# Softmax attention scores from float32r parts in two row tiles, in place of bfloat16 parts over the whole array

## The reference, cut to what matters

```python
q, k, v = split(x @ qkv_w.T + qkv_b)            # 16 heads, HD = 8
scores  = einsum('bhqe,bhke->bhqk', q, k) / sqrt(8)
attn    = softmax(scores, axis=-1)              # over 2048 keys
out     = einsum('bhqk,bhke->bhqe', attn, v)
out     = out.reshape(b, s, d) @ proj_w.T + proj_b
```

## Time and profile before

| | us |
|---|---|
| runs shown, median of 3 | 1872.74 (1870.85 to 1875.92) |
| the profiled execution | 1868.55 |
| its span in the trace | 1866.7 |
| mean granted TensorE clock | 0.928 of full |
| PE busy in the span | 1628.6 (87%) |
| DVE busy | 1353.9 (73%) |
| ACT busy | 837.3 (45%) |

### The profile page before, as it was taken

One profiled execution on the slowest core, in us unless ns is written; L12 is line 12 of the kernel. 1 busy time (PEld: TensorE's weight loads), 2 busy tenths in 40 slices (PEclk: granted clock), 3 DMA queues, 4 the chain that ended last, 5 costly groups with the idle time before them and its releaser, 6 DMA issues. The chain is left out here.

```text
span 1866.7 us, 21571 instructions
## 1 busy us (share of the span) xinstructions
PE 1628.6 (87%) x7272; PEld 684.2 (37%) x7285; DVE 1353.9 (73%) x1951; ACT 837.3 (45%) x1493; POOL 222.5 (12%) x145
## 2 busy tenths in 40 slices
PE   6987589999999999999998888899994446589999
PEld 3433212222222222222221533366661112256665
DVE  5776788888888888888870686656657999745654
ACT  2433427767767667677677343322223000042222
POOL 2222300000000000000000022211101324301110
PEclk8998659999999999999999899899996777799999
DMA  6000410012001110011000000000000000000000
GB/s 169 3 0 1 123 29 8 15 27 40 8 10 31 27 21 6 27 27 23 2 1 2 1 0 0 0 1 1 0 1 0 0 1 0 1 1 6 6 6 6
DMA packets 32016, 29.42 MB, mean 16 GB/s; under 512 B 7788, under 2 KB 27032, under 8 KB 31928
## 3 DMA queue, kind: packets, MB, share of 16 engines
q1 hardware_dynamic: 31928, 28.31, 6.1%
HBM read 22.13 MB, written 4.19 MB: 14 GB/s over the span
## 5 line engine op out<-in xcount | busy, mean ns | idle before, releaser
L1382 DVE TENSOR_REDUCE mx<-ps 128x1 f32<-128x1024 f32 x512 | 604.5, 1220 | 134.2 <-PE ps L1269 130.8
L1269 PE MATMUL ps<-k,q 72*128 72x512 bf16 x1024 | 401.9, 407 | 26.7 <-PEq L967 14.9
L1304 PE MATMUL ps<-q,k 84*128 84x512 bf16 x1024 | 344.4, 382 | 14.6 <-ACT xn L1359 11.7
L1359 ACT ACTIVATE xT<-ps 128x512 f32<-128x512 f32 x512 | 265.2, 601 | 149.6 <-PE ps L1304 149.6
L1359 ACT ACTIVATE xn<-ps 128x512 f32<-128x512 f32 x512 | 266.2, 601 | 102.5 <-PE ps L1304 102.5
L1269 PEld LDWEIGHTS ps<-k,q 72*128 72x128 bf16 x1024 | 109.6, 115 | 333.0 <-DVE mx L1382 184.4
L854 ACT ACTIVATE silu<-ps 128x512 f32<-128x512 f32 x144 | 85.3, 596 | 265.2 <-PE ps L827 261.9
L1304 PEld LDWEIGHTS ps<-q,k 84*128 84x128 bf16 x1024 | 102.5, 102 | 171.1 <-ACT xn L1359 63.4
L889 DVE TENSOR_TENSOR hid<-ps,silu 128x512 f32<-128x512 f32 x144 | 97.8, 689 | 91.1 <-PE ps L831 89.4
L827 PE MATMUL ps<-xT,ew 128*128 (+1 forms) x288 | 151.0, 606 | 6.5 <-PEq L1750 4.8
L817 PEld LDWEIGHTS ps<-ew,hid 128*128 128x128 f32 x1152 | 138.7, 192 | 30.6 <-issue 29.9
(11 more groups left out here) (238 smaller groups left out, 1686.4 us busy)
## 6 DMA issues: line engine op xcount, KB each, us to landing
k<-k_parts SPq DMA_DIRECT2D x90, 64.0 KB
q<-q_parts SPq DMA_DIRECT2D x144, 32.0 KB
k<-k_parts SPq DMA_DIRECT2D x108, 32.0 KB
ew<-in_L_ffn_w_dram SPq DMA_DIRECT2D x2, 1024.0 KB
wraw<-in_L_ffn_w_dram SPq DMA_DIRECT2D x3, 512.0 KB, 6.8
q_parts<-part SPq DMA_DIRECT2D x4, 384.0 KB, 4.3
k_parts<-part SPq DMA_DIRECT2D x4, 384.0 KB, 2.6
v<-values SPq DMA_DIRECT2D x8, 144.0 KB, 5.0
```

Source lines behind the costliest of these rows:

```text
L1269: mm = nc.tensor.matmul(m.ps[:, S1B[i % 4], :], queries, k1[:, h, kc * CHUNK:(kc + 1) * CHUNK], start=True, stop=True)
L1304: nc.tensor.matmul(m.ps[:, S2_BANK[s], :], k2[:, h, kt * P:(kt + 1) * P], q[:, qc, h, :], start=True, stop=True).then_inc(s2_ready, 1)
L1359: nc.scalar.activation(ex[kt % P_RING][:, h, :], m.ps[:, S2_BANK[s], :], ACT.Exp).then_inc(exped, 1)
L1382: nc.vector.reduce_max(mx[:, h, qt, kc:kc + 1], m.ps[:, 2 * (i % 2):2 * (i % 2) + 2, :], AX.XY)\
```

## The change

Queries and keys are split into two float32 parts: the value with its low 12 bits cleared (`bitwise_and` with -4096), and the rest. A head then needs 4 products of parts, 32 rows, and 8 further rows carry the maxima (two parts of four heads). They are kept as float32r. Two heads lie in one tile: one at partitions 0 to 39, the other at 64 to 103 (ROW_TILE = 64), so a first pass is a pair of matmuls into two banks, one in either half of the array's rows, and one `reduce_max` with two outputs takes both. Scores of even heads use the lower rows, those of odd heads the upper ones. The maxima are split in two parts on DVE; 8 DMAs take them instead of 4.

The order on PE is new: scores stand three steps ahead of the tile's `weigh`, which now takes the tile's own exponentials, and first passes come as pairs in 32 places a unit (LEAD = 8 places, HOLE = 1). During the start 14 further matmuls on zeros (`warm`) stand between first passes. In the parts stage DVE clears the bits, POOL subtracts, and ACT no longer copies; eight one-column `affine_select`s make `own_row` at its start.

```diff
-LEAD = 12
-HOLE = 3
+LEAD = 8
+HOLE = 1
-    q = m.sb("q", [ROWS_M, CHUNKS, GH, CHUNK], BF16, stack=kv_stack)
-    k1 = m.sb("k1", [ROWS, GH, T], BF16, stack=kv_stack)
+    q = m.sb("q", [P, CHUNKS, PAIRED, CHUNK], F32R, stack=kv_stack)
+    k1 = m.sb("k1", [P, PAIRED, T], F32R, stack=kv_stack)
...
+            for h in range(GH):
+                for i in range(PARTS2):
+                    row = h % 2 * ROW_TILE + ROWS + i * GH + h
+                    own(nc.gpsimd.affine_select(out=own_row[:, h // 2:h // 2 + 1], ...
+            for n in range(len(jobs)):
+                low_part(n)      # POOL: full - high part, float32, 512 columns
...
-        S2_BANK = [S2B[s % 3] for s in range(STEPS - 1)] + [S2B[1]]
+        SLOTS = 2 * TILES
+        done = [max(0, (k + 1 - HOLE) * PAIRS // (SLOTS - HOLE)) for k in range(-1, SLOTS)]
+        S1_IN = [range(done[k], done[k + 1]) for k in range(SLOTS)]
...
+            def load_maxima(u):
+                sp.wait_ge(max_turned, u + 1)
+                for b in range(P // 32):
+                    rows = neg_turned[b * 32:b * 32 + PARTS2 * GH, :, :].rearrange("r j t -> r (j t)").unsqueeze(1)\
+                        .to_broadcast([PARTS2 * GH, PAIRED, P])
+                    for p in range(2):
+                        at = p * ROW_TILE + ROWS
+                        sp.dma_start(q[at:at + PARTS2 * GH, u % CHUNKS, :, b * P:(b + 1) * P].bitcast(F32), rows)\
+                            .then_inc(max_loaded, 16)
...
+            def first_pass(u, i):
+                g, qc = u // CHUNKS, u % CHUNKS
+                kc, qt, pair = i // (PAIRS // CHUNKS), i // 2 % TPC, i % 2
...
+                if u > 0 or i >= 2:
+                    pe.wait_ge(s1_used, u * PAIRS + i - 1)
+                for p in range(2):
+                    rows = slice(p * ROW_TILE, p * ROW_TILE + ROWS)
+                    queries = q[rows, qc, pair, :].rearrange("r (p t) -> r t p", t=TPC)[:, qt, :]
+                    mm = nc.tensor.matmul(m.ps[:, S1B[2 * pair + p], :], queries, k1[rows, pair, kc * CHUNK:(kc + 1) * CHUNK],
+                                          start=True, stop=True)
+                mm.then_inc(s1_ready, 1)
...
+            def score(n):
+                u, s = n // STEPS, n % STEPS
+                g, qc, kt, h = u // CHUNKS, u % CHUNKS, s // GH, s % GH
+                if s == 0:
+                    pe.wait_ge(max_loaded, DMAS_M * (u + 1))
...
+                if n >= len(S2B):
+                    pe.wait_ge(exped, n - len(S2B) + 1)
+                rows = slice(h % 2 * ROW_TILE, h % 2 * ROW_TILE + ROWS_M)
+                nc.tensor.matmul(m.ps[:, S2B[n % len(S2B)], :], k2[rows, h // 2, kt * P:(kt + 1) * P], q[rows, qc, h // 2, :],
+                                 start=True, stop=True).then_inc(s2_ready, 1)
...
+            for i in range(PAIRS):
+                first_pass(0, i)
+            for i in range(S1_IN[LEAD].start):
+                warm()
+                warm()
+                first_pass(1, i)
+            pe.wait_ge(own_stored, 4)
+            for n in range(len(S2B)):
+                score(n)
+            for u in range(UNITS):
                 for kt in range(TILES):
+                    n = u * STEPS + kt * GH
+                    score(n + 3)
+                    ahead(u, 2 * kt)
+                    score(n + 4)
+                    score(n + 5)
+                    score(n + 6)
+                    ahead(u, 2 * kt + 1)
+                    weigh(u, kt)
...
-                    nc.vector.reduce_max(mx[:, h, qt, kc:kc + 1], m.ps[:, 2 * (i % 2):2 * (i % 2) + 2, :], AX.XY)\
+                    nc.vector.reduce_max(mx[:, 2 * pair:2 * pair + 2, qt, kc], m.ps[:, 2 * pair:2 * pair + 2, :], AX.X)\
                         .then_inc(s1_used, 1)
```

More of the change, by code:

```diff
@@ L6 @@
 BF16 = mybir.dt.bfloat16
+F32R = mybir.dt.float32r
+I32 = mybir.dt.int32
 ALU = mybir.AluOpType
@@ L957, in softmax_attention @@
     zeros = m.sb("zeros", [P, CHUNK], BF16, stack=kv_stack)
[L958 to L963, removed]
+    key_rows = dram_k.rearrange("j (g s p e) t -> j g p e s t", g=GROUPS, s=PAIRED, p=2)
@@ L1018, in _ @@
                 if n >= 2:
-                    act.wait_ge(parts_ready, n - 1)
+                    act.wait_ge(lo_ready, n - 1)
                 nc.scalar.activation(full[:, n % 2, :], m.ps[:, n % 2, :], ACT.Identity, bias=m.qk_bias[:, s:s + 1],
                                      scale=sides[s][1]).then_inc(f32_ready, 1)
[L1022 to L1025, removed]
         @block.vector
         def _(dve):
-            step = Chain(dve, steps)
+            step = Chain(dve, m.sem("norm_steps"))
             norm.all_chunks(step)
@@ L1096, in softmax_attention @@
     q_loaded = [m.sem(f"q_loaded{i}") for i in range(CHUNKS)]
-    k1_loaded = [m.sem(f"k1_loaded{i}") for i in range(GH)]
+    k1_loaded = [m.sem(f"k1_loaded{i}") for i in range(CHUNKS)]
     k2_loaded = [m.sem(f"k2_loaded{i}") for i in range(2)]
@@ L1130, in softmax_attention @@
[L1130 to L1145, removed]
@@ L1147, in load_k2, with load_k1 @@
-        def load_k2(eng, g, half):
[L1148 to L1152, removed]
+        DMAS_M = 16 * 2 * (P // 32)
+        DMAS_R = 16 * 8
+        def load_k1(eng, g, kc):
+            load_keys(eng, k1, g, slice(kc * CHUNK, (kc + 1) * CHUNK), k1_loaded[kc])
@@ L1154, in load_v @@
+        def load_k2(eng, g, half):
+            load_keys(eng, k2, g, slice(half * (T // 2), (half + 1) * (T // 2)), k2_loaded[half])
         def load_v(eng, g, half):
@@ L1274, in weigh @@
-            def weigh(g, qc, kt, first=False):
-                u = g * CHUNKS + qc
+            def first_pass(u, i):
+                g, qc = u // CHUNKS, u % CHUNKS
+                kc, qt, pair = i // (PAIRS // CHUNKS), i // 2 % TPC, i % 2
+                if i == 0 and u > 0:
+                    pe.wait_ge(q_loaded[qc], DMAS_R * (g + 1 if qc > 0 else g))
+                if qc == 0 and g > 0 and i % (PAIRS // CHUNKS) == 0:
+                    pe.wait_ge(k1_loaded[kc], DMAS_R * g)
+                if u > 0 or i >= 2:
+                    pe.wait_ge(s1_used, u * PAIRS + i - 1)
+                for p in range(2):
+                    rows = slice(p * ROW_TILE, p * ROW_TILE + ROWS)
[3 more added lines that the diff above has]
+                mm.then_inc(s1_ready, 1)
@@ new lines, in ahead @@
+            def ahead(u, slot):
+                v = u + 1 + (slot + LEAD) // SLOTS
+                if v < UNITS:
+                    for i in S1_IN[(slot + LEAD) % SLOTS]:
+                        first_pass(v, i)
+            def score(n):
+                if n >= UNITS * STEPS:
+                    return
+                u, s = n // STEPS, n % STEPS
+                g, qc, kt, h = u // CHUNKS, u % CHUNKS, s // GH, s % GH
+                if s == 0:
+                    pe.wait_ge(max_loaded, DMAS_M * (u + 1))
+                if qc == 0 and h == 0 and kt % (TILES // 2) == 0:
+                    pe.wait_ge(k2_loaded[kt // (TILES // 2)], DMAS_R * (g + 1))
+                if n >= len(S2B):
[3 more added lines that the diff above has]
+                                 start=True, stop=True).then_inc(s2_ready, 1)
@@ L1277, in weigh @@
+            def weigh(u, kt):
+                g, qc = u // CHUNKS, u % CHUNKS
                 if qc == 0 and kt % (TILES // 2) == 0:
                     pe.wait_ge(v_loaded[kt // (TILES // 2)], 16 * (g + 1))
-                if kt == 0 and not first:
+                if kt == 0 and u > 0:
                     pe.wait_ge(out_stored, u)
@@ L1286, in weigh @@
                 last.then_inc(av_done, 1)
-            def unit(g, qc, last, first=False):
-                u = g * CHUNKS + qc
-                after = [(g, qc + 1), (g, qc + 2)]
-                after = [(a, b) if b < CHUNKS else (a + 1, b - CHUNKS) for a, b in after]
-                def ahead(s):
-                    if last and (qc == CHUNKS - 1 or (qc == CHUNKS - 2 and s + LEAD >= STEPS)):
-                        return
-                    for i in S1_IN[(s + LEAD) % STEPS]:
-                        first_pass(*after[(s + LEAD) // STEPS], i)
-                def score(s):
-                    kt, h = s // GH, s % GH
-                    if not (first and s < len(S2B)):
-                        pe.wait_ge(exped, u * STEPS + (s - S2_SINCE[s] + 1))
-                    nc.tensor.matmul(m.ps[:, S2_BANK[s], :], k2[:, h, kt * P:(kt + 1) * P], q[:, qc, h, :],
-                                     start=True, stop=True).then_inc(s2_ready, 1)
-                pe.wait_ge(max_loaded, DMAS_M * (u + 1))
-                for kt in range(TILES):
-                    if qc == 0 and kt % (TILES // 2) == 0:
-                        pe.wait_ge(k2_loaded[kt // (TILES // 2)], DMAS_K * (g + 1))
-                    s = kt * GH
-                    score(s)
-                    score(s + 1)
-                    ahead(s)
-                    score(s + 2)
-                    ahead(s + 1)
-                    score(s + 3)
```

(69 more changed lines are left out.)

213 lines of the change are left out of this document (90 added, 123 removed).

## The result

The changed kernel takes 2422.09 us (4 runs, 2419.41 to 2423.35) against 1871.99: a ratio of 1.2932, 95% interval 1.2909 to 1.2954. The forecast was 1805. The profiled execution has a span of 2417.7 us at a mean granted clock of 0.675 (before 0.928).

The account below looks back on a forecast made before the run. PE was taken to bound the kernel, then the exponential's loop: units of 43.15 us against 47.93 save 71.7; ends add 2, parts stage 1.5, so -68.2 gives 1800.3 profiled, 1805 us predicted; range 1780 to 1850.

Parts of the forecast that it names:

- the third rival: Score stage: PE's clock stays at 0.50, a kt takes 4.1 us, the time is near 2160 us; chance 0.05.
- The price of a half clock: Score stage at half clock: the loop through the exponential takes 4.1 us a kt, U = 66, time near 2160 us.
- The switches: Tiling-mode changes between first passes and scores: two more a kt, one adding 0.1 us, 24 us in all; not in the sum.
- One pass per matmul: Score stage: a float32r matmul of 512 columns takes 0.215 us, like a bfloat16 one; bounds 0.215 and 0.86.
- The load: float32r weight load on PE: at worst one shows in the loop, 0 to 0.1 us; half of the worst case taken.
- The second rival: Score stage: a float32r matmul takes 0.43 us, 3.25 us a kt, time 1956 us; chance 0.13 for 0.43 or more.
- Row halves side by side: First passes: two matmuls in two row halves take 0.22 us a pair; bounds 0.22 side by side, 0.43 in line.
- The first rival: First passes: the row halves do not run side by side, a pair takes 0.43 us, time 1847 us; chance 0.12.
- The loop as the new bound: Score stage: exponential, score, pair, `weigh`, score sets the pace at 2.60 us a kt, 2.65 taken; bounds 2.60 and 2.80.
- The maxima's way: Between units: DMAs land the maxima 4.7 to 8.2 us after the turn, 5.5 taken; 5.6 are left, so nothing added.
- the fourth rival: Unit starts: maxima come late, 1.8 us a unit, or tile modes switch; time 1829 to 1832 us, joint chance 0.12.
- The eight selects: Parts stage: POOL's selects of 0.68 us each delay the first rstd about 2 us; stage taken at +1.5, bounds -3 to +5.

Follow-up runs that it names:

- the one of 2258 us: The changed kernel with first passes over 40 rows instead of 32, the added rows zeros, so they match the scores' rows: 2258.45 us, a single run.
- 1848: The changed kernel with first passes and scores over all 64 rows of their half, the added rows zeros: 1848.20 us, ratio to before 0.9888.

## Why the prediction was wrong

The failed step is the argument against the third rival, "The clock stays at half", which got it a chance of 0.05: that PE as busy as it would be here gets the full clock. The runs showed 0.50 with PE busy 99.7 of 100 us, because of the rows that its matmuls use. The 617 us between 1805 and 2422 fall in three parts, each a difference of two measured kernels (the first: of one and the forecast; the one of 2258 us is a single run): 1848 - 1805 = 43, 2258 - 1848 = 410, 2422 - 2258 = 164. Two lines of the kernel before, from the stretch that held the clock with PE busy 6.7 of 10 us and from the last matmuls before the fall, show what rows those had:

```profile
1086.07 1.10 PE L577 MATMUL ps<-hid,wT 128*128 128x512 f32 x2 [0.95 <-DVE prod L711]
...
1470.12 5.70 PE L1664 MATMUL ps<-xT,v_rep 128*128 128x512 f32 x8 [8.04 <-DVE kv L1700]
```

- **The clock, 410 us.** I set against it that PE without a gap took the clock to 1.00, that it fell only without matmuls, and that it held at 6.7 of 10 us busy. All three stretches have matmuls of 72 rows or more. I carried over the busy time and not the rows. The earlier trace rows already said that busy time is not all: PE busy 38 of 46 us over 72 rows, at 0.50 throughout, a larger share than the 6.7 of 10 at 1.00. The Trainium skill (TensorE: Matmul & The Clock Gate, "Why this matters for your kernels") advises keeping TensorE busy without pause to get the full clock; here it was busy 99.7 of 100 us at half, so the measurement decides against busy time as the whole rule.
- **The price of a half clock** was 2160, too low by 262. I priced the exponential's loop (4.1 us), but in the changed kernel PE's own sum is longer, 5.19, switches in it. Without the switches (the kernel of 2258 us) the loop does set the pace, and at 4.45: score to exponential is 0.83 and score to `weigh` 1.15, where I had 0.65 and 0.96, worked out from bfloat16 rows.
- **The switches, 164 us.** The sum had none; a rival had two more a kt at 0.1, from the rule in the Trainium skill (TensorEngine Tiling (Array Packing), Key Properties) and a bfloat16 row. The trace agrees with the rule if 32 rows are one mode and 40 and 64 another: with 40 and 40 rows or 40 and 64 the gap goes, with 32 and 40 it is there. But there are three more a kt, not two. The price was right in bfloat16 (0.11) and too low by a factor of three in float32r at half clock, two at full clock (0.21).
- **float32r, 43 us.** One pass per matmul was right: a pair takes 0.81 at half clock where two passes would be over 1.0. The load was bounded at 0.1 once in the loop, and 0.05 taken; the type costs 0.23, in two places. The second rival is refuted.
- **Row halves side by side:** right (0.81 for two, 0.79 for one), which agrees with the rule on distinct row groups in the Trainium skill (TensorE: Matmul & The Clock Gate, Part 3). The first rival is refuted.
- **The loop as the new bound:** not in the changed kernel, where PE's sum binds. With 64 rows it is right, to 0.01 us in bfloat16 (2.59 for 2.60). Moving the pair out took away what the forecast said it cost.
- **The maxima's way:** their eight DMAs are issued in 6.03, 0.75 each, near the upper end. No score of the changed kernel waited for them, but only because its kts are long: at 2.59 a kt they land some 7.0 after the turn where I took 5.5, and come late by 0.9 us a unit (13.3 in all), as the fourth rival says, at half its price.
- **Small terms.** The eight selects take 2.77 us, not 5.4; the parts stage ends at 216.9 instead of 218.5, so -1.6 where +1.5 was taken. The 14 `warm` matmuls did not lift the clock: it is 0.50 behind them, so "PE enters the units warm" was wrong as well.

## What to carry to other kernels

Count the rows a matmul uses when you ask which clock it will get: here row tiles saved PE work and the few rows in them halved its clock, and padding the contraction with zero rows, which did not lengthen a unit (at full clock 46.5 us with scores of 40 rows, 46.2 with 64), brought it back. When work is moved to row tiles, give neighbouring matmuls the same tile, and keep out of the loop between a consumer and the next producer whatever need not be there. A rival told by a column of the profile (here the clock) must be checked against rows that resemble the new work, not only the new load.

## What the runs showed of the hardware that was not expected

- The granted clock stood at 0.50 with PE busy 100 of 100 us (32 and 40 rows of bfloat16, plain order), and at 1.00 with PE busy 91 of 100 over 64 rows, of which 24 (scores) or 32 (first passes) were zeros. What more the clock follows is open.
- 32-row and 40-row matmuls cost a switch between them (0.11 us in bfloat16, about 0.3 in float32r, both at half clock), 40-row and 64-row ones none.
- At full clock a float32r weight load of 128 columns takes 0.18 us (0.28 at half clock), a bfloat16 one 0.09; where a score had to wait, its exponential starts 0.53 after it instead of 0.42.
